# Global attention: two units at a time on every engine, in place of one

## The chip, the cores and the metric

The kernel runs on one NeuronCore of a Trainium2 chip. The metric is the device time of one execution in microseconds, the median of several. The engines, each with its own instruction queue worked strictly in order, are TensorE (PE, with its weight loads PEld), VectorE (DVE), ScalarE (ACT), GpSimd (POOL) and SyncE (SP, which issues transfers here). They meet through semaphores.

## The reference

Four layers follow one another on a tensor of 4 images, 64 x 64 positions, 128 channels. The change concerns the second, a single-head attention of every position over all 4096 positions of its image:

```python
h = group_norm(x, gn_scale, gn_bias)            # 32 groups of 4 channels
hf = h.reshape(B, N, C)                         # N = 4096, C = 128
q, k, v = hf @ wq + bq, hf @ wk + bk, hf @ wv + bv
w_ = jnp.einsum('bqd,bkd->bqk', q, k) * C ** (-0.5)
w_ = jax.nn.softmax(w_, axis=2)
o = jnp.einsum('bqk,bkd->bqd', w_, v)
o = o @ wo + bo
return x + o.reshape(B, H, W, C)
```

The first layer is an attention over 7 x 7 neighbours, the third a gated product with row sums, the fourth a convolution with a selective scan. They run before and after this stage and aren't touched.

## The kernel before

`layer1` computes this attention for four images in one stream. Products of single precision are made from a high and a low part (tiles ending in h and l): `three` (L697 to L700) issues high x high, low x high, high x low.

For each image the queries are 32 blocks of 128. A block's scores over 4096 keys are 8 units of 512 keys, so an image has 256 score units, and all four have STEPS = 1024. The weights have to be turned before they can be multiplied with the values. For that two blocks form a group, and a group has 16 units: unit V turns 256 queries by 256 keys (four transposes, L777) and multiplies them with the values (six matmuls, L789 to L791).

All engines walk through the same list of steps, from -30 to STEPS + 3. In step t there are:

- TensorE: the scores of unit t + 24 into one of three score banks (`psS`), the turn of unit t + 1 into one of two banks (`psT`), the product with the values of unit t. After every 16 steps, in step 16m + 3, two output matmuls (L801).
- VectorE: the maximum of score unit t + 24 (L963, it also copies the scores to `pr`; the last of eight is followed by two small operations for the row), and the low part `pl` of the turned unit t + 1 (L974), which needs the high part. In step 16m + 3 the finish of a group (L981 to L989).
- ScalarE: the high part `ph` of the turned unit t + 1 (L864), then the exponential of unit t + 16 (L869). In step 16m + 1 a copy of the output sums (L875).

A turn waits for `pl` of the unit two before it, a product with the values for its own `pl`, a score for its bank, which the maximum gives back.

Work for the next image stands at the head of certain steps, planned in `at` (L533 to L553), and is done by every engine ahead of the step's own. With base = 256b for image b: the load and turning of a chunk ("raw", "channels") every 22 steps from base - 244 on; the moments of the normalisation in steps base - 66 to base - 62, with a square root on ScalarE; and, for eight chunks each, "norm" (a load), two steps later "normal" (high part `nh` on ScalarE, an affine operation on VectorE, low part `nl` on GpSimd), two steps after that "product". Products of kind 0 give k and q of a chunk, are in the eight steps from base - 26, one in each, and take two score banks. Products of kind 1 give v, are in every second step from base - 14, and take one. In a product TensorE fills a bank, ScalarE makes the high part of k, q or v (`kh`, `qh`, `vh`), VectorE the low part (`kl`, `ql`, `vl`) and gives the bank back. The banks are handed out in the order of use, three in turn (`bank`, L562). `xc` (loads), `nh` and `nl` have two buffers each.

Of the kernel before, what the change touches and what calls it, by code (L numbers as in the profile page):

```python
# [8 lines left out]
ALU = mybir.AluOpType  # L9
# [3 lines left out]
NI = 4  # L13
# [472 lines left out]
def layer1(nc, io, x1, x1t, x2):  # L486
    with ExitStack() as ctx:
# [50 lines left out]
        for b in range(NI):  # L538
# [7 lines left out]
            for kind, first, every in ((0, -26, 1), (1, -14, 2)):  # L546
                for ch in range(8):
# [1 line left out]
                    plan(t, "product", b, ch, kind)  # L549
                    plan(t - 2, "normal", b, ch, kind)  # L550
                    plan(t - 4, "norm", b, ch, kind)
        for jobs in at.values():
            jobs.sort(key=lambda j: ("product", "normal", "channels", "moments", "norm", "raw").index(j[0]))  # L553
        steps = range(-30, STEPS + 4)
        first = [("channels", 0, ch) for ch in range(8)] + [("moments", 0, k) for k in range(3)]


# [40 lines left out]

        for job in first:
            order(job)  # L600
        for step in steps:
            for job in at.get(step, ()):
                order(job)
            if 0 <= step + 24 < STEPS:
                bank("s", step + 24)
        normals = {job[1:]: i for i, job in enumerate(j for s in steps for j in at.get(s, ()) if j[0] == "normal")}
        products = {job[1:]: i for i, job in enumerate(j for s in steps for j in at.get(s, ()) if j[0] == "product")}
        splits = {}
# [85 lines left out]
        def tensor(e):  # L694
# [52 lines left out]
                channels(0, ch)  # L747
            for k in (1, 2):
                fold(0, k)
            for step in steps:  # L750
                for what, *a in at.get(step, ()):
                    if what == "channels":
                        channels(*a)
                    elif what == "moments" and a[1]:
                        fold(*a)
                    elif what == "product":
                        product(*a)
                U = step + 24
                if 0 <= U < STEPS:
                    b, (q, kc) = U // 256, divmod(U % 256, 8)  # L760
                    i = S_use["s", U][1]
                    qs, ks = slice(128 * q, 128 * q + 128), slice(512 * kc, 512 * kc + 512)
                    for ch in (kc, q // 4):
                        _, bk, turn = S_use["q", b, ch]
                        w.wait_ge(S_free[bk], turn + 1)
                    S_wait(w, "s", U)
                    three(psS[:, i, :], qh[:, qs], ql[:, qs], kh[:, ks], kl[:, ks]).then_inc(S_full, 1)
                V = step + 1
                if 0 <= V < STEPS:
                    i, g, j = V % 2, V // 16, V % 16  # L770
                    if V >= 2:
                        w.wait_ge(p_lo, V - 1)
                    for q in range(2):
                        w.wait_ge(exped, 8 * (2 * g + q) + j // 2 + 1)
                        for k in range(2):
                            kt = 2 * j + k
                            t = e.transpose(psT[:, i, 256 * k + 128 * q:256 * k + 128 * q + 128], pr[:, (2 * g + q) % 5, 128 * kt:128 * kt + 128], ident[:])  # L777
                    t.then_inc(T_full, 1)
                if 0 <= step < STEPS:
                    b, j, i, G = step // 256, step % 16, step % 2, step // 16  # L780
                    out = psO[:, G % 2, 0:256]
                    w.wait_ge(p_lo, step + 1)
                    if G >= 2:
                        w.wait_ge(o_out, G - 1)
                    _, bk, turn = S_use["v", b, j // 2]
                    w.wait_ge(S_free[bk], turn + 1)
                    for k in range(2):
                        kt, ks = 2 * j + k, slice(256 * k, 256 * k + 256)
                        e.matmul(out, vh[:, kt, :], ph[:, i, ks], start=(j == 0 and k == 0), stop=False)  # L789
                        e.matmul(out, vl[:, kt, :], ph[:, i, ks], start=False, stop=False)  # L790
                        t = e.matmul(out, vh[:, kt, :], pl[:, i, ks], start=False, stop=(j == 15 and k == 1))  # L791
                    t.then_inc(pv_done, 1)
                if step % 16 == 3 and step > 16:
                    G = step // 16 - 1
                    w.wait_ge(o_out, G + 1)
                    if G:
                        w.wait_ge(y_done, 2 * G)
                    else:
                        w.wait_ge(bob_done, 1)
                    for q in range(2):  # L800
                        t = e.matmul(psF[:, 128 * q:128 * q + 128], ots[:, 128 * q:128 * q + 128], wraw[:, 3, :], start=True, stop=True)  # L801
                    t.then_inc(F_full, 1)

        def scalar(e):
# [40 lines left out]
            for ch in range(8):  # L845
                channels(0, ch)
            root(0)
            for step in steps:
                for what, *a in at.get(step, ()):
# [8 lines left out]
                V = step + 1  # L858
                if 0 <= V < STEPS:
                    i = V % 2  # L860
                    w.wait_ge(T_full, V + 1)
                    if V >= 2:
                        w.wait_ge(pv_done, V - 1)
                    e.activation(ph[:, i, :], psT[:, i, :], ACT.Copy).then_inc(p_hi, 1)  # L864
                Q, k = divmod(step + 16, 8)
                if 0 <= Q < 32 * NI:
                    s, es = Q % 5, slice(512 * k, 512 * k + 512)
                    w.wait_ge(maxed, 2 * Q + 2)
                    e.activation(pr[:, s, es], pr[:, s, es], ACT.Exp, bias=st[:, s, 9:10], scale=SC, accum_out=st[:, s, 10 + k:11 + k]).then_inc(exped, 1)  # L869
                if step % 16 == 1 and step > 16:  # L870
                    G = step // 16 - 1
                    w.wait_ge(pv_done, 16 * G + 16)
                    if G:
                        w.wait_ge(F_full, G + 1)
                    e.activation(ots[:], psO[:, G % 2, 0:256], ACT.Copy).then_inc(o_out, 1)  # L875

        def vector(e):
# [42 lines left out]
            def product(b, ch, kind):  # L920
# [6 lines left out]
                else:  # L927
                    bk, sl4 = S_use["v", b, ch][1], slice(4 * ch, 4 * ch + 4)
                    w.wait_ge(hi_done, splits["v", b, ch] + 1)
                    e.tensor_tensor(vl[:, sl4, :], psS[:, bk, :].rearrange("p (t c) -> p t c", c=128), f32(vh[:, sl4, :]), ALU.subtract).then_inc(S_free[bk], 1)  # L930

            e.memset(zero[:], 0.0)
            w.wait_ge(weights, 192)
            e.tensor_copy(wh[:], wraw[:, 0:3, :]).then_inc(w_hi, 1)
# [5 lines left out]
                channels(0, ch)  # L940
            for k in range(3):
                fold(0, k)
            for step in steps:
                for what, *a in at.get(step, ()):
# [8 lines left out]
                U = step + 24  # L953
                if 0 <= U < STEPS:
                    (Q, kc), ks = divmod(U, 8), slice(512 * (U % 8), 512 * (U % 8) + 512)
                    s = Q % 5
                    u, bk, turn = S_use["s", U]
                    w.wait_ge(S_full, u + 1)
                    if Q >= 5:
                        w.wait_ge(T_full, 16 * ((Q - 5) // 2) + 16)  # L960
                    elif s == 4:
                        w.wait_ge(S_full, 8)
                    e.tensor_tensor_reduce(pr[:, s, ks], psS[:, bk, :], zero[:].broadcast_to([128, 512]), 1.0, -3.0e38,  # L963
                                           ALU.add, ALU.max, st[:, s, kc:kc + 1]).then_inc(S_free[bk], 1)
                    if kc == 7:
                        w.wait_ge(S_free[bk], turn + 1)
                        e.tensor_reduce(st[:, s, 8:9], st[:, s, 0:8], AX.X, ALU.max).then_inc(maxed, 1)
                        w.wait_ge(maxed, 2 * Q + 1)
                        e.tensor_scalar(st[:, s, 9:10], st[:, s, 8:9], -SC, None, ALU.mult).then_inc(maxed, 1)  # L969
                V = step + 1  # L970
                if 0 <= V < STEPS:
                    i = V % 2
                    w.wait_ge(p_hi, V + 1)
                    e.tensor_tensor(pl[:, i, :], psT[:, i, :], f32(ph[:, i, :]), ALU.subtract).then_inc(p_lo, 1)  # L974
                if step % 16 == 3 and step > 16:
                    G = step // 16 - 1
                    for q in range(2):
                        n = 2 * G + q
                        s = n % 5
# [1024 lines left out]
```

## Time and profile before

| | |
|---|---|
| three runs | 4606.60, 4616.47, 4618.91 us; median 4616.47 |
| the profiled execution | 4611.34 us, its span 4609.5 us |
| mean granted clock of TensorE | 0.891 of full speed |
| busy share of the span: PE, DVE, ACT, POOL | 84%, 74%, 58%, 30% |
| this attention, by its first and last product with values | 898.9 to 2909.1 us |

The shares are means over four layers with different limits. What a change in one of them is worth has to be read in that stretch alone, by its waits and its timeline.

### The profile page before, as it was taken

What the parts mean: (1) busy time and instruction counts of PE and PEld (TensorE: products, weight loads), DVE (VectorE), ACT (ScalarE), POOL (GpSimd) and SP (SyncE); (2) the same over time, 40 slices, a digit from 0 to 9 for tenths busy, and PEclk for the clock granted to TensorE, in tenths of its full rate; (3) what the DMA queues carried; (4) which work ended last, traced back from release to release, by engine and by line L of the source; (5) the groups of instructions that cost most, each with busy time, mean ns of one, the idle gap of its engine ahead of it and who ended that gap; (6) DMA issues with size and microseconds to landing.
All of it is one profiled execution on the core that took longest, in us unless ns stands there. A gap on an engine that the chain in (4) does not pass through costs nothing. (4 is left out here: it accounts for less than half of the span.)

```text
span 4609.5 us, 73934 instructions
## 1 busy us (share of the span) xinstructions
PE 3873.8 (84%) x25590; PEld 2996.1 (65%) x25590; DVE 3406.9 (74%) x7889; ACT 2678.2 (58%) x6018; POOL 1391.3 (30%) x1373
## 2 busy tenths in 40 slices
PE   6888887799999999999999999676999644455579
PEld 4666665699988998899888998444666311111148
DVE  4666666577787777777787777695666798899934
ACT  3666665577776777767776667333222466666621
POOL 2434443100010000200010000112244599999910
PEclk9999999799999999999999999898999755555579
DMA  7777774200010000100010000212222311122143
GB/s 205 204 199 198 197 198 137 76 24 21 18 37 27 20 24 16 42 24 24 17 39 13 10 10 10 67 62 95 77 77 71 145 55 55 60 69 71 58 151 102
DMA packets 274687, 346.40 MB, mean 75 GB/s; under 512 B 34954, under 2 KB 159754, under 8 KB 272778
## 3 DMA queue, kind: packets, MB, share of 16 engines
q1 hardware_dynamic: 261738, 320.55, 22.8%
q0 software_dynamic: 12288, 16.92, 1.4%
q8 instruction: 205, 3.36, 0.3%
q10 hardware_dynamic: 288, 4.19, 0.2%
q14 instruction: 168, 1.38, 0.1%
HBM read 209.58 MB, written 130.02 MB: 74 GB/s over the span
## 5 line engine op out<-in xcount | busy, mean ns | idle before, releaser
L864 ACT ACTIVATE l_ph<-l_T 128x512 fp32r<-128x512 f32 x1024 | 612.4, 598 | 547.2 <-PE l_T L777 547.2
L974 DVE TENSOR_TENSOR l_pl<-l_T,l_ph 128x512 fp32r<-128x512 f32 x1024 | 707.3, 691 | 274.9 <-ACT l_ph L864 274.2
L963 DVE CUSTOM_DVE_ANT_0 l_pr<-l_S,l_zero 128x512 f32<-128x512 f32 x1024 | 704.7, 689 | 74.1 <-PE l_S L700 11.2
L869 ACT ACTIVATE l_pr<-l_pr,l_st 128x512 f32<-128x512 f32 x1024 | 731.5, 714 | 1.1 <-DVE l_st L969 1.0
L789 PE MATMUL l_O<-l_ph,l_vh 128*128 128x256 f32 x2048 | 661.7, 323 | 12.2 <-DVE l_pl L974 12.1
L777 PE MATMUL l_T<-l_ident,l_pr 128*128 128x128 f32 x4096 | 612.8, 272 | 0.0
L777 PEld LDWEIGHTS l_T<-l_ident,l_pr 128*128 128x128 f32 x4096 | 507.6, 140 | 136.2
L790 PE MATMUL l_O<-l_ph,l_vl 128*128 128x256 f32 x2048 | 577.9, 282 | 0.0
L791 PE MATMUL l_O<-l_pl,l_vh 128*128 128x256 f32 x2048 | 576.8, 282 | 0.0
L1005 POOL TENSOR_TENSOR l_xs<-l_xs,l_bob 128x128 f32<-128x128 f32 x128 | 57.1, 461 | 1644.7 <-DMA l_xs<-x 1643.6
L1658 PE MATMUL l3b_C<-l_D,l_sel 32*128 32x512 f32 x256 | 216.4, 845 | 384.5 <-DVE l3b_E L1716 384.1
L1658 PEld LDWEIGHTS l3b_C<-l_D,l_sel 32*128 32x128 f32 x256 | 72.4, 283 | 601.4 <-DVE l3b_E L1716 598.2
L698 PE MATMUL l_S<-l_kh,l_qh 128*128 128x512 f32 x1024 | 417.6, 408 | 1.1 <-DVE l_st L963 0.6
L1739 POOL TENSOR_TENSOR l_acc<-l_acc,l3b_E 128x512 f32<-128x512 f32 x256 | 403.4, 1576 | 40.7 <-DVE l3b_E L1716 35.4
L789 PEld LDWEIGHTS l_O<-l_ph,l_vh 128*128 128x128 f32 x2048 | 388.8, 190 | 28.2 <-DVE l_pl L974 24.1
L699 PE MATMUL l_S<-l_kh,l_ql 128*128 128x512 f32 x1024 | 406.8, 397 | 0.0
L700 PE MATMUL l_S<-l_kl,l_qh 128*128 128x512 f32 x1024 | 404.3, 395 | 0.0
L790 PEld LDWEIGHTS l_O<-l_ph,l_vl 128*128 128x128 f32 x2048 | 388.8, 190 | 0.0
L791 PEld LDWEIGHTS l_O<-l_pl,l_vh 128*128 128x128 f32 x2048 | 385.8, 188 | 0.0
L1713 DVE TENSOR_TENSOR_SCAN l3b_du<-l3b_L,l3b_du 128x512 f32<-128x512 f32 x256 | 325.6, 1272 | 23.4 <-POOL l3b_du L1750 20.7
L1695 ACT ACTIVATE l3b_E<-l3b_d 128x512 f32<-128x512 f32 x256 | 153.0, 598 | 237.1 <-PE l3b_d L1664 236.9
L433 DVE CUSTOM_DVE_ANT_0 l_pr<-l_S,l_bm 128x308 f32<-128x308 f32 x512 | 237.2, 464 | 57.5 <-PE l_S L309 47.4
(241 smaller groups left out, 8842.7 us busy)
## 6 DMA issues: line engine op xcount, KB each, us to landing
hls<-l_hl SPq DMA_DIRECT2D x64, 512.0 KB, 4.7
l_qs<-hls SPq DMA_DIRECT2D x96, 256.0 KB, 3.8
l_ks<-hls SPq DMA_DIRECT2D x96, 256.0 KB, 4.0
l_xc<-x1t SPq DMA_DIRECT2D x64, 256.0 KB, 2.7
zs<-l3a_tmp SPq DMA_DIRECT2D x64, 256.0 KB, 2.0
l3b_z<-zs SPq DMA_DIRECT2D x64, 256.0 KB, 2.8
yz<-l3b_z SPq DMA_DIRECT2D x64, 256.0 KB, 2.0
l3c_y<-yz SPq DMA_DIRECT2D x16, 1024.0 KB, 17.1
```

Of the source, the lines that this page charges most:

```text
L698: e.matmul(out, lh, rh, start=True, stop=False)
L699: e.matmul(out, ll, rh, start=False, stop=False)
L700: return e.matmul(out, lh, rl, start=False, stop=True)
L777: t = e.transpose(psT[:, i, 256 * k + 128 * q:256 * k + 128 * q + 128], pr[:, (2 * g + q) % 5, 128 * kt:128 * kt + 128], ident[:])
L789: e.matmul(out, vh[:, kt, :], ph[:, i, ks], start=(j == 0 and k == 0), stop=False)
L790: e.matmul(out, vl[:, kt, :], ph[:, i, ks], start=False, stop=False)
L791: t = e.matmul(out, vh[:, kt, :], pl[:, i, ks], start=False, stop=(j == 15 and k == 1))
L864: e.activation(ph[:, i, :], psT[:, i, :], ACT.Copy).then_inc(p_hi, 1)
L869: e.activation(pr[:, s, es], pr[:, s, es], ACT.Exp, bias=st[:, s, 9:10], scale=SC, accum_out=st[:, s, 10 + k:11 + k]).then_inc(exped, 1)
L963: e.tensor_tensor_reduce(pr[:, s, ks], psS[:, bk, :], zero[:].broadcast_to([128, 512]), 1.0, -3.0e38, ALU.add, ALU.max, st[:, s, kc:kc + 1 ...
L974: e.tensor_tensor(pl[:, i, :], psT[:, i, :], f32(ph[:, i, :]), ALU.subtract).then_inc(p_lo, 1)
L1739: e.tensor_tensor(o, o, turned(tE[:, m % 5, :], n ^ a4), ALU.add).then_inc(added, 1)
```

## The change

Every engine walks through pairs of steps. In a pair p (even) the jobs of both steps come first, then TensorE issues the scores of units p + 24 and p + 25, the products with the values of units p and p + 1, and the turns of units p + 2 and p + 3. VectorE does two maxima, then two low parts; ScalarE two high parts, then two exponentials. The banks are handed out in that order. The output matmuls and the group's finish move from step 16m + 3 to the end of pair 16m + 2, the copy of the sums from step 16m + 1 to pair 16m. SyncE and GpSimd keep their lists of single steps; their own order isn't changed. The inner parts of `scores`, `turn`, `attend` and `maximum` are the lines of before.

```diff
+        pairs = range(-30, STEPS + 4, 2)
+        def jobs(pair):
+            return at.get(pair, []) + at.get(pair + 1, [])
...
-        for step in steps:
-            for job in at.get(step, ()):
+        for pair in pairs:
+            for job in jobs(pair):
                 order(job)
-            if 0 <= step + 24 < STEPS:
-                bank("s", step + 24)
+            for U in (pair + 24, pair + 25):
+                if 0 <= U < STEPS:
+                    bank("s", U)
...
         def tensor(e):
+            for pair in pairs:
+                for what, *a in jobs(pair):
...
-                U = step + 24
-                if 0 <= U < STEPS:
...
-                V = step + 1
-                if 0 <= V < STEPS:
...
-                if 0 <= step < STEPS:
...
-                if step % 16 == 3 and step > 16:
-                    G = step // 16 - 1
+                for U in (pair + 24, pair + 25):
+                    if 0 <= U < STEPS:
+                        scores(U)
+                for V in (pair, pair + 1):
+                    if 0 <= V < STEPS:
+                        attend(V)
+                for V in (pair + 2, pair + 3):
+                    if 0 <= V < STEPS:
+                        turn(V)
+                if pair % 16 == 2 and pair > 16:
+                    G = pair // 16 - 1
...
         def scalar(e):
+                for V in (pair + 2, pair + 3):
...
                     e.activation(ph[:, i, :], psT[:, i, :], ACT.Copy).then_inc(p_hi, 1)
+                for Q, k in (divmod(pair + 16, 8), divmod(pair + 17, 8)):
...
                     e.activation(pr[:, s, es], pr[:, s, es], ACT.Exp, ...).then_inc(exped, 1)
-                if step % 16 == 1 and step > 16:
+                if pair % 16 == 0 and pair >= 16:
...
         def vector(e):
+                for U in (pair + 24, pair + 25):
+                    if 0 <= U < STEPS:
+                        maximum(U)
+                for V in (pair + 2, pair + 3):
+                    if 0 <= V < STEPS:
+                        i = V % 2
+                        w.wait_ge(p_hi, V + 1)
+                        e.tensor_tensor(pl[:, i, :], psT[:, i, :], f32(ph[:, i, :]), ALU.subtract).then_inc(p_lo, 1)
+                if pair % 16 == 2 and pair > 16:
```

## Rows read from the trace of the kernel before

**Rows 1.** Windows: us, busy of PE, PEld, DVE, ACT, POOL, then PE clock, DMA share, GB/s

```profile
898.89:2909.07 2010.18, 1997.97 (x14024) 1795.52 (x14022) 1579.09 (x3828) 1430.76 (x3255) 117.86 (x174) 1.00 0.08 22
1340.27:1346.71 6.44, 6.44 (x41) 5.58 (x39) 6.31 (x15) 6.44 (x13) 2.61 (x2) 1.00 0.22 60
```

**Rows 2.** Waits of weight loads, 898.9 to 2909.1 us: total, times, longest

```profile
PEld l_O L789 <- DVE l_pl L974: 24.1, 51, 1.5
```

**Rows 3.** Timeline of a plain step: start us, us, engine, line, operation

```profile
1552.33 0.60 PE L777 MATMUL l_T<-l_ident,l_pr 128*128 128x128 f32 x4
1552.68 0.36 PE L789 MATMUL l_O<-l_ph,l_vh 128*128 128x256 f32 x1
1552.88 0.28 PE L790 MATMUL l_O<-l_ph,l_vl 128*128 128x256 f32 x1
1552.96 0.60 ACT L864 ACTIVATE l_ph<-l_T 128x512 fp32r<-128x512 f32 x1 [0.56 <-PE l_T L777]
...
1553.45 0.71 ACT L869 ACTIVATE l_pr<-l_pr,l_st 128x512 f32<-128x512 f32 x1
1553.48 0.40 PE L698 MATMUL l_S<-l_kh,l_qh 128*128 128x512 f32 x1
1553.59 0.69 DVE L974 TENSOR_TENSOR l_pl<-l_T,l_ph 128x512 fp32r<-128x512 f32 x1 [0.37 <-ACT l_ph L864]
...
1554.53 0.36 PE L789 MATMUL l_O<-l_ph,l_vh 128*128 128x256 f32 x1
```

**Rows 4.** Costliest groups of the page: count | busy, mean ns | idle before

```profile
L963 DVE CUSTOM_DVE_ANT_0 l_pr<-l_S,l_zero 128x512 f32<-128x512 f32 x1024 | 704.7, 689 | 74.1 <-PE l_S L700 11.2
...
L777 PE MATMUL l_T<-l_ident,l_pr 128*128 128x128 f32 x4096 | 612.8, 272 | 0.0
```

**Rows 5.** Timeline at a group's finish

```profile
1540.68 0.15 DVE L981 TENSOR_REDUCE l_st<-l_st 128x1 f32<-128x8 f32 x1
...
1542.04 0.68 DVE L963 CUSTOM_DVE_ANT_0 l_pr<-l_S,l_zero 128x512 f32<-128x512 f32 x1
...
1542.94 0.60 PE L777 MATMUL l_T<-l_ident,l_pr 128*128 128x128 f32 x4
1543.39 0.39 PE L789 MATMUL l_O<-l_ph,l_vh 128*128 128x256 f32 x1
```

**Rows 6.** Timeline beside products of kind 0

```profile
1341.15 0.69 ACT L836 ACTIVATE l_kh<-l_S,l_cols 128x512 fp32r<-128x512 f32 x1
...
1341.88 0.75 DVE L926 SCALAR_TENSOR_TENSOR l_kl<-l_S,l_cols,l_kh 128x512 fp32r<-128x512 f32 x1
...
1343.14 0.58 ACT L864 ACTIVATE l_ph<-l_T 128x512 fp32r<-128x512 f32 x1
...
1346.36 0.59 ACT L864 ACTIVATE l_ph<-l_T 128x512 fp32r<-128x512 f32 x1
```

**Rows 7.** Timeline beside products of kind 1, in the first image and in a change

```profile
876.38 0.60 ACT L842 ACTIVATE l_vh<-l_S 128x512 fp32r<-128x512 f32 x1 [2.17 <-PE l_S L700]
...
877.71 0.55 DVE L918 TENSOR_SCALAR l_xc<-l_xc,l_gs 128x512 f32<-128x512 f32 x1
...
878.34 1.27 POOL L999 TENSOR_TENSOR l_nl<-l_xc,l_nh 128x512 fp32r<-128x512 f32 x1 [3.60 <-DVE l_xc L918]
...
1381.27 0.19 PEld L789 LDWEIGHTS l_O<-l_ph,l_vh 128*128 128x128 f32 x1 [0.40 <-DVE l_pl L974]
...
1386.72 0.19 PEld L789 LDWEIGHTS l_O<-l_ph,l_vh 128*128 128x128 f32 x1 [0.40 <-DVE l_pl L974]
```

**Rows 8.** Timeline of the last steps

```profile
2880.93 0.38 PE L789 MATMUL l_O<-l_ph,l_vh 128*128 128x256 f32 x1 [0.23 <-DVE l_pl L974]
...
2881.75 0.60 PE L777 MATMUL l_T<-l_ident,l_pr 128*128 128x128 f32 x4
...
2883.76 0.39 PE L789 MATMUL l_O<-l_ph,l_vh 128*128 128x256 f32 x1 [0.22 <-DVE l_pl L974]
```

More of the change, by code:

```diff
@@ L551, in layer1 @@
                     plan(t - 4, "norm", b, ch, kind)
-        for jobs in at.values():
-            jobs.sort(key=lambda j: ("product", "normal", "channels", "moments", "norm", "raw").index(j[0]))
+        for todo in at.values():
+            todo.sort(key=lambda j: ("product", "normal", "channels", "moments", "norm", "raw").index(j[0]))
         steps = range(-30, STEPS + 4)
+        pairs = range(-30, STEPS + 4, 2)
+        def jobs(pair):
+            return at.get(pair, []) + at.get(pair + 1, [])
         first = [("channels", 0, ch) for ch in range(8)] + [("moments", 0, k) for k in range(3)]
@@ L749, in tensor, with scores, turn, attend @@
                 fold(0, k)
-            for step in steps:
-                for what, *a in at.get(step, ()):
+            def scores(U):
+                b, (q, kc) = U // 256, divmod(U % 256, 8)
+                i = S_use["s", U][1]
+                qs, ks = slice(128 * q, 128 * q + 128), slice(512 * kc, 512 * kc + 512)
+                for ch in (kc, q // 4):
+                    _, bk, turn = S_use["q", b, ch]
+                    w.wait_ge(S_free[bk], turn + 1)
+                S_wait(w, "s", U)
+                three(psS[:, i, :], qh[:, qs], ql[:, qs], kh[:, ks], kl[:, ks]).then_inc(S_full, 1)
+            def turn(V):
+                i, g, j = V % 2, V // 16, V % 16
+                if V >= 2:
+                    w.wait_ge(p_lo, V - 1)
+                for q in range(2):
+                    w.wait_ge(exped, 8 * (2 * g + q) + j // 2 + 1)
+                    for k in range(2):
+                        kt = 2 * j + k
+                        t = e.transpose(psT[:, i, 256 * k + 128 * q:256 * k + 128 * q + 128], pr[:, (2 * g + q) % 5, 128 * kt:128 * kt + 128], ident[:])
+                t.then_inc(T_full, 1)
+            def attend(V):
+                b, j, i, G = V // 256, V % 16, V % 2, V // 16
+                out = psO[:, G % 2, 0:256]
+                w.wait_ge(p_lo, V + 1)
+                if G >= 2:
+                    w.wait_ge(o_out, G - 1)
+                _, bk, turn_ = S_use["v", b, j // 2]
+                w.wait_ge(S_free[bk], turn_ + 1)
+                for k in range(2):
+                    kt, ks = 2 * j + k, slice(256 * k, 256 * k + 256)
+                    e.matmul(out, vh[:, kt, :], ph[:, i, ks], start=(j == 0 and k == 0), stop=False)
+                    e.matmul(out, vl[:, kt, :], ph[:, i, ks], start=False, stop=False)
+                    t = e.matmul(out, vh[:, kt, :], pl[:, i, ks], start=False, stop=(j == 15 and k == 1))
+                t.then_inc(pv_done, 1)
+            for pair in pairs:
+                for what, *a in jobs(pair):
                     if what == "channels":
@@ L757, in tensor @@
                         product(*a)
-                U = step + 24
-                if 0 <= U < STEPS:
[L760 to L767, printed above, removed]
@@ L768, in tensor @@
-                V = step + 1
-                if 0 <= V < STEPS:
[L770 to L778, printed above, removed]
@@ L779, in tensor @@
-                if 0 <= step < STEPS:
[L780 to L792, printed above, removed]
@@ L847, in scalar @@
             root(0)
-            for step in steps:
-                for what, *a in at.get(step, ()):
+            for pair in pairs:
+                for what, *a in jobs(pair):
                     if what == "channels":
@@ L857, in scalar @@
                         product(*a)
[L858 to L869, printed above, removed]
[L870 to L871 removed]
+                for V in (pair + 2, pair + 3):
+                    if 0 <= V < STEPS:
+                        i = V % 2
+                        w.wait_ge(T_full, V + 1)
+                        if V >= 2:
+                            w.wait_ge(pv_done, V - 1)
+                        e.activation(ph[:, i, :], psT[:, i, :], ACT.Copy).then_inc(p_hi, 1)
+                for Q, k in (divmod(pair + 16, 8), divmod(pair + 17, 8)):
+                    if 0 <= Q < 32 * NI:
+                        s, es = Q % 5, slice(512 * k, 512 * k + 512)
+                        w.wait_ge(maxed, 2 * Q + 2)
+                        e.activation(pr[:, s, es], pr[:, s, es], ACT.Exp, bias=st[:, s, 9:10], scale=SC, accum_out=st[:, s, 10 + k:11 + k]).then_inc(exped, 1)
+                if pair % 16 == 0 and pair >= 16:
+                    G = pair // 16 - 1
                     w.wait_ge(pv_done, 16 * G + 16)
@@ L930, in product, with maximum @@
                     e.tensor_tensor(vl[:, sl4, :], psS[:, bk, :].rearrange("p (t c) -> p t c", c=128), f32(vh[:, sl4, :]), ALU.subtract).then_inc(S_free[bk], 1)
+            def maximum(U):
+                (Q, kc), ks = divmod(U, 8), slice(512 * (U % 8), 512 * (U % 8) + 512)
+                s = Q % 5
+                _, bk, turn = S_use["s", U]
+                w.wait_ge(S_full, S_use["s", U][0] + 1)
+                if Q >= 5:
+                    w.wait_ge(T_full, 16 * ((Q - 5) // 2) + 16)
+                elif s == 4:
+                    w.wait_ge(S_full, 8)
+                e.tensor_tensor_reduce(pr[:, s, ks], psS[:, bk, :], zero[:].broadcast_to([128, 512]), 1.0, -3.0e38,
+                                       ALU.add, ALU.max, st[:, s, kc:kc + 1]).then_inc(S_free[bk], 1)
+                if kc == 7:
+                    w.wait_ge(S_free[bk], turn + 1)
+                    e.tensor_reduce(st[:, s, 8:9], st[:, s, 0:8], AX.X, ALU.max).then_inc(maxed, 1)
+                    w.wait_ge(maxed, 2 * Q + 1)
+                    e.tensor_scalar(st[:, s, 9:10], st[:, s, 8:9], -SC, None, ALU.mult).then_inc(maxed, 1)
             e.memset(zero[:], 0.0)
@@ L942, in vector @@
                 fold(0, k)
-            for step in steps:
-                for what, *a in at.get(step, ()):
+            for pair in pairs:
+                for what, *a in jobs(pair):
                     if what == "channels":
@@ L952, in vector @@
                         product(*a)
[L953 to L976, printed above, removed]
+                for U in (pair + 24, pair + 25):
+                    if 0 <= U < STEPS:
+                        maximum(U)
+                for V in (pair + 2, pair + 3):
+                    if 0 <= V < STEPS:
+                        i = V % 2
+                        w.wait_ge(p_hi, V + 1)
+                        e.tensor_tensor(pl[:, i, :], psT[:, i, :], f32(ph[:, i, :]), ALU.subtract).then_inc(p_lo, 1)
+                if pair % 16 == 2 and pair > 16:
+                    G = pair // 16 - 1
                     for q in range(2):
```

## The prediction

> **What bounds the kernel now.** I read the busy shares by stretch first, then the waits of TensorE, then single steps in the timeline. Names: S is a score unit (three matmuls of 512 columns, L698 to L700), T a turn (four transposes, L777), A a product with the values (six matmuls of 256 columns, L789 to L791); ph and pl are the high and low part of the turned weights (ScalarE L864, VectorE L974), E an exponential (L869), M a maximum (L963). A "step" is one S, T and A.
>
> In the stage's 2010.18 us TensorE is busy 1997.97 [rows 1], and it waits for pl 24.1 us in 51 waits that the view lists [rows 2]. The busy share alone doesn't say that the stream is dense, so I take a step apart [rows 3]. From A at 1552.68 to the next A at 1554.53 are 1.85 us. T and A together take 1552.33 to 1553.48 = 1.15, which leaves S 0.70. The four transposes take 0.60 in all and one of them 0.27 [rows 4], so they start (0.60 - 0.27)/3 = 0.11 apart and T takes 0.44. That leaves A 0.71, 0.118 for each of six. So three stages of dense issue add up to the step: TensorE is the bound, with nothing idle in a plain step.
>
> **Does the order itself cost anything on TensorE?** This decides whether pairing can save at all. The first A starts at 1552.68, only 0.03 after the last transpose (1552.33 + 3 x 0.11 = 1552.66), and the second matmul of A starts 0.20 after the first instead of 0.12. Read alone, the 0.20 looks like a cost of 0.08 for going from T to A. But 0.03 + 0.20 = 0.23 is what one transpose and one A matmul take anyway (0.11 + 0.12). The first A enters early and the gap behind it pays back. At the rows' digits a change of kind costs 0.00 to 0.01; the other end is the 0.08. I take 0.006, by the sum that closes (two changes in a pair become one, 512 pairs): -3 us.
>
> **Plain pairs.** Let X be the start of T(p+2); T(p+3) follows at X+0.44, S, S at X+0.87 and X+1.57, A(p+2) at X+2.27, A(p+3) at X+2.98, the next T at X+3.70. From [rows 3]: ph starts 0.63 after T, holds ScalarE 0.49; pl starts 0.63 after ph and takes 0.69. So pl(p+2) ends at X+0.63+0.63+0.69 = X+1.95, and A(p+2) could start some 0.06 later: 0.26 to spare. pl(p+3) ends by X+2.6, A(p+3) starts at 2.98. Before, A starts 1554.53 - 1552.33 = 2.20 after its T, so the spare was 0.19: the pair is no tighter. VectorE runs pl, pl until X+2.55, then M, M (0.69 each at most [rows 4]) until X+3.93, and is wanted at X+3.70+1.26 = X+4.96. ScalarE runs ph, ph, E, E: X+0.63, 1.12, 1.61, 2.32 (E 0.71), free at X+3.03. Both are ahead. Cost: 0.
>
> **The row finish of each group** (64 of them): VectorE is held 1542.04 - 1540.68 = 1.36 us [rows 5]; now an A that follows starts 0.45 after its T instead of 0.35, 0.10 lost, plus what follows. In the pair VectorE ends this work and two M at X+2.55+1.36+1.38 = X+5.29, and pl is wanted at X+3.70+0.22 (the two output matmuls)+1.26 = X+5.18: 0.11 late, within the 0.26. The wait goes, -6.4 us for 64. (Where the four transposes of a chunk of the next image fall in such a pair a wait of some 0.2 stays, in either order: 0.)
>
> **Products of the next image, kind 0 (k and q).** There are eight of these in each of three image changes, one per step. They run past the previous image's attention. Here the other engines are the limit too: in 6.44 us, two steps, ScalarE is busy 6.44 and VectorE 6.31 [rows 1]. The product uses two of the three score banks, each bank needing TensorE, ScalarE, VectorE in turn. In a pair the order is k, q, k', q', S, S', A, A, T, T, on three banks. q' needs the bank of k, S' that of k'. ScalarE starts with E, E of the pair before and reaches kh only at X+3.03; then, by [rows 6], kh, qh and nh hold it 1343.14 - 1341.15 = 1.99, so kh' starts at X+5.02. kl' starts 0.73 after kh' and takes 0.75: X+6.50. S' starts at X+6.56, takes 0.70 and after a wait about 0.1 more (its second matmul starts late), then A, A 1.42: the next T is at X+8.78. ScalarE had run out of work at X+7.0 (q'h, n'h) and waits until X+8.78+0.63 for the next T: its next jobs stand behind ph in its queue. Before: 3.22 per step (ph at 1343.14 to ph at 1346.36), 6.44 per two. So +2.34 for each of three pairs; the last pair has no nh: kl' behind ql ends at X+5.9, next T at X+8.18, +1.74. Per image 8.8, three images +26.3. Bounds per image: 0 if ScalarE caught up somehow (the row has it 100% busy, so a gap can't be made good), and +12 if the burst also cost what late loads may add, some 0.8 (about an nh) in each of four pairs. I take the worked-out value. The first image has no ph or E beside these products; I take 0 with 3 us either way, since its waits are on loads.
>
> **The two normal parts ahead of them** (steps -28, -27) fall in one pair: ScalarE holds VectorE back with two nh (some 0.7 each, a third of the 1.99, until X+4.5); the second affine (0.55 [rows 7]) and M, M follow, so pl(p+2) starts near X+6.35 instead of 4.96, less the 0.26 to spare: 1.1 lost, where I count 0.5 for the two steps of before (between none and 1.1). +1.8 us, between -1.5 and +3.3.
>
> **Products of kind 1 (v)**, every second step, so one per pair, 24 beside attention. Before, 5.45 us per pair of steps (1381.27 to 1386.72) with a wait of 0.40 [rows 7], so 5.05 without. The chain v high, nh, affine, nl is now behind two E instead of one: vh at X'+3.03, affine 1.33 later, nl 0.63 after that, 1.27 long: nl is there at X'+6.26, the next v at X'+6.31. v is wanted at X+0.87, and X is X'+5.05 plus the wait w that v itself had: 6.31 = 5.05 + 0.87 + 2w gives w = 0.20 and a pair of 5.25. So 0.20 less, 24 times: -4.8 us. The wait on pl goes and a shorter one on nl takes its place.
>
> **The three table loads** (square root between exponentials): longest wait 1.5 [rows 2], 1.2 in the pair by the same working (0.26 to spare instead of 0.19, and VectorE comes out of pl, pl earlier): -1 us.
>
> **The last 24 steps have no S to cover the turn.** Before, two of them take 2.83 us (2880.93 to 2883.76) [rows 8]: A(V) still runs between T(V+1) and A(V+1). In pairs nothing does: T to its A takes 2.01 (2881.75 to 2883.76), the first A 0.82 with its late second matmul (2880.93 to 2881.75), the second 0.71: 3.54. Twelve pairs: 12 x (3.54 - 2.83) = 8.5, less about 1.5 at the ends (one T of 0.44 is counted in, the group finish no longer adds): +7.
>
> **Sum.** 26.3 + 7 + 1.8 - 1 - 4.8 - 6.4 - 3 = +19.9, so +20 us. The profiled execution took 4611.34 us (span 4609.5, 1.8 around it), which gives 4631. The median of the three timed runs is 4616.47, 5 above it; with that base 4636. I say 4635. The order and the sizes of all other stages stay.
>
> **A rule against the change.** In a plain step 0.44 of 1.85 us are transposes and the granted clock is 1.00 over the whole stage [rows 1, 3], the 2.4 GHz level. The Trainium skill ("TensorE: Matmul & The Clock Gate", Part 4: PE-mode transpose) says that transposes don't count as busy for the clock in the way other matmuls do. The pair puts 0.87 us of them in a row, and in the last 24 steps 1.15 us of waiting behind them: if the clock fell to 1.2 GHz there, T and A would take twice as long, 12 x (0.87 + 1.53) = 29 us more, 4664. By that rule; the trace speaks against it, since the last steps of before, with a third of their time in transposes, kept 2.4 GHz. Chance 0.02.
>
> **Rivals.** (a) The bursts cost little: ScalarE's queue is not as far behind as I count, or loads and maxima shift so that k', q' meet free banks; then 7 + 1.8 stand against savings of 15.2: 4616.5 - 6.4 = 4610. Against it: ScalarE's 6.44 of 6.44. Chance 0.15. (b) The other side: grouping removes real cost on TensorE. If the 0.08 behind T were a cost of changing kind, one less per pair is 512 x 0.08 = 41 us, net -21: 4595. It decides from the point where T+A in a row is longer than its parts by over 0.04; the rows have 0.23 against 0.23. Chance 0.06. (c) Plain pairs are not free: if M, M ahead of pl, or ph(p+3) behind ph(p+2), leave A waiting 0.1 in each of some 480 plain pairs, +48 us: 4684. For it: 0.26 to spare is little. Against: VectorE is free 1.0 us before pl is wanted. Chance 0.09. (d) The pair does half of what I say in the bursts (+13 instead of +26): 4622. Chance 0.13. My forecast: 0.55.
>
> **Chances.** No change can be told within 0.3%, 14 us of 4616: 4603 to 4630. Slower: the forecast's own case nearly whole (its range is 4628 to 4645), (c), the clock: 0.68. Same: (d), most of (a), the edge of the forecast: 0.23. Faster: (b) and a tail of (a): 0.09. The range 4608 to 4658 leaves out (b), (c) and the clock.
>
> **What would show it.** In the profile after: plain pairs of 3.70 us from T to T with no wait of A; in the image changes four pairs of some 8.8, 8.8, 8.8, 8.2 us, ScalarE idle some 2.3 in each before ph, waiting for T; value pairs of 5.25; the last pairs 3.54. I am wrong if plain pairs differ from 3.70 by over 0.03 (15 us over the stage), or if the pairs with k and q take under 7.5.

## The result, and the profile after

The changed kernel takes 4633.6 us (median of 8 runs, 4624.36 to 4644.89), the kernel before 4615.23 us (median of 8, 4605.12 to 4620.09). The ratio is 1.0044, with a 95% interval of 1.003 to 1.0058: slower by 18 us. That is 0.44%, clear of no difference at all, and the interval's lower end lies at the 0.3% that the prediction counts as no change. 4635 was forecast.

The profiled execution of after is its slowest, 4644.89 us with a span of 4643.1, so its 33.6 us above the span of before are more than the medians differ. I compare the stage itself, and it stretch by stretch, by the starts of ph. From ph(0) to ph(1022) the stage takes 2010.30 us before and 2029.85 after: +19.55, where +19.9 was worked out for the whole. This measure leaves out both ends. From the stage's first statistics (812.95 and 816.31) to the end of its last result on VectorE (2911.57 and 2932.95) it is 2098.62 before and 2116.64 after: +18.0. The pairs gain 0.6 ahead of ph(0) and 0.95 behind ph(1022): the last ph starts 0.50 after its neighbour in after and 1.68 in before. The other 15.5 us of the two spans lie in layers whose code is the same (last section).

First the busy times of after by stretch (columns: us of the stretch, busy us and instructions of PE, PEld, DVE, ACT, POOL, granted clock, DMA share, GB/s), beside [rows 1]: the stage up to its last product with values, less its first 0.2 us, one pair with products of kind 0, one plain pair, and the last pairs.

```profile
902.28:2930.44 2028.16, 1992.55 (x14017) 1838.47 (x14016) 1474.52 (x3826) 1373.93 (x3254) 117.82 (x174) 1.00 0.08 22
1345.55:1354.18 8.63, 7.01 (x42) 5.50 (x39) 6.29 (x12) 6.30 (x13) 2.58 (x2) 1.00 0.21 60
1550.98:1554.67 3.69, 3.69 (x28) 3.44 (x27) 3.18 (x10) 2.49 (x7) 0.86 (x2) 1.00 0.46 129
2888.63:2927.65 39.02, 28.73 (x226) 26.16 (x225) 15.34 (x28) 19.22 (x43) 0.92 (x2) 1.00 0.03 8
```

The plain pair is full: PE 3.69 of 3.69. In the pair with products ScalarE, which was busy 6.44 of 6.44, has 6.30 of 8.63, and PE has 7.01. In the last pairs PE has 28.73 of 39.02. The granted clock is 1.00 in all.

The waits of weight loads after, beside [rows 2] (us in total, times, longest):

```profile
PEld l_S L704 <- DVE l_kl L942: 25.6, 21, 1.9
PEld l_O L787 <- DVE l_pl L993: 19.7, 24, 1.2
PEld l_S L704 <- POOL l_nl L1018: 10.3, 18, 1.3
```

Two of the three are new: a product or score for a bank that kl gives back, and a product for nl. What was 24.1 us in 51 waits for pl is 19.7 in 24, with the last pairs in it.

A plain pair, beside [rows 3] (start, us, engine, line, operation, and in brackets the idle time before and who ended it):

```profile
1550.98 1.09 ACT L880 ACTIVATE l_ph<-l_T 128x512 fp32r<-128x512 f32 x2 [1.65 <-PE l_T L774]
1551.61 1.29 DVE L993 TENSOR_TENSOR l_pl<-l_T,l_ph 128x512 fp32r<-128x512 f32 x2 [0.27 <-ACT l_ph L880]
1552.60 0.28 PE L787 MATMUL l_O<-l_ph,l_vh 128*128 128x256 f32 x1
1554.03 1.03 PE L774 MATMUL l_T<-l_ident,l_pr 128*128 128x128 f32 x8
1554.67 1.09 ACT L880 ACTIVATE l_ph<-l_T 128x512 fp32r<-128x512 f32 x2 [1.20 <-PE l_T L774]
```

A stands without a wait, and ph comes again after 3.69. The first pl starts at 1551.61 and one takes 0.69, so it ends at 1552.30, 0.30 ahead of the A at 1552.60. With the 0.06 that the prediction allows for the hand-over, 0.24 is to spare, where 0.26 was worked out.

A pair with products of kind 0, beside [rows 6]:

```profile
1344.75 1.04 PE L774 MATMUL l_T<-l_ident,l_pr 128*128 128x128 f32 x8
1345.39 1.09 ACT L880 ACTIVATE l_ph<-l_T 128x512 fp32r<-128x512 f32 x2 [2.26 <-PE l_T L774]
1347.77 0.68 ACT L852 ACTIVATE l_kh<-l_S,l_cols 128x512 fp32r<-128x512 f32 x1
1348.49 0.75 DVE L942 SCALAR_TENSOR_TENSOR l_kl<-l_S,l_cols,l_kh 128x512 fp32r<-128x512 f32 x1 [1.18 <-ACT l_kh L852]
1349.29 0.50 PE L704 MATMUL l_S<-l_nh,l_wh 128*128 128x512 f32 x1 [1.42 <-DVE l_kl L942]
1349.62 0.69 ACT L852 ACTIVATE l_kh<-l_S,l_cols 128x512 fp32r<-128x512 f32 x1
1351.15 0.51 PE L704 MATMUL l_S<-l_kh,l_qh 128*128 128x512 f32 x1 [0.19 <-DVE l_kl L942]
1353.38 1.03 PE L774 MATMUL l_T<-l_ident,l_pr 128*128 128x128 f32 x8
1354.02 1.09 ACT L880 ACTIVATE l_ph<-l_T 128x512 fp32r<-128x512 f32 x2 [2.33 <-PE l_T L774]
```

With X = 1344.75: kh at X+3.02 (3.03 was worked out), kh' at X+4.87 (5.02), S' at X+6.40 (6.56), the next T at X+8.63 (8.78), ScalarE idle 2.33 ahead of ph (2.3). TensorE's long wait, 1.42, is for q', the second product's last matmuls, on the bank that the first kl gives back.

The last pairs, beside [rows 8]:

```profile
2899.27 1.08 ACT L880 ACTIVATE l_ph<-l_T 128x512 fp32r<-128x512 f32 x2 [1.06 <-PE l_T L774]
2899.90 1.29 DVE L993 TENSOR_TENSOR l_pl<-l_T,l_ph 128x512 fp32r<-128x512 f32 x2 [2.26 <-ACT l_ph L880]
2900.64 0.39 PE L787 MATMUL l_O<-l_ph,l_vh 128*128 128x256 f32 x1 [0.98 <-DVE l_pl L993]
2902.18 1.04 PE L774 MATMUL l_T<-l_ident,l_pr 128*128 128x128 f32 x8
2902.82 1.08 ACT L880 ACTIVATE l_ph<-l_T 128x512 fp32r<-128x512 f32 x2 [1.07 <-PE l_T L774]
```

ph to ph is 3.55 (3.54 was worked out), with TensorE waiting 0.98 for pl in each but one: there, two output matmuls stand between, and the wait is 0.53.

The whole stage by stretches, from the start of ph of the first unit named to that of the last. Rows with "x3" are sums over the three image changes. H2 and H3 are two experiments below. In the first row, some 1 us isn't the work of an edit: the first eight steps take 17.36 us in after and E1 and 16.29 in E2, though these three do the same there. Before (17.07) and after both have the long value, H2 (16.08) and H3 (15.95) the short one.

| stretch of steps | before | after | H2 | H3 |
|---|---|---|---|---|
| 0 to 192, plain with 11 finishes | 367.13 | 365.54 | 363.63 | 365.92 |
| moments, 192 to 198, x3 | 40.46 | 39.05 | 39.20 | 47.14 |
| 198 to 226, x3 | 157.55 | 156.47 | 156.42 | 156.76 |
| two nh, 226 to 230, x3 | 23.65 | 23.46 | 23.46 | 23.67 |
| k and q, 230 to 238, x3 | 78.94 | 103.37 | 81.54 | 79.46 |
| 238 to 242, x3 | 22.34 | 22.12 | 22.12 | 21.88 |
| v, 242 to 258, x3 | 132.25 | 130.77 | 122.35 | 133.36 |
| plain, 258 to 448 and 514 to 704 | 723.17 | 719.38 | 718.12 | 723.15 |
| 770 to 1000 | 433.39 | 430.66 | 430.67 | 433.33 |
| 1000 to 1022, no scores | 31.42 | 39.03 | 31.69 | 31.43 |
| total | 2010.30 | 2029.85 | 1989.20 | 2016.11 |

### The profile page after: what moved, and what is told of

Same layout as the page of the kernel before. It is cut to its first block and busy times, and to the rows that moved or that the text cites. A ratio compares the mean times of both kernels' runs of the same rounds, so it can differ in the third digit from the quotient of the medians.

```text
span 4643.1 us, 73934 instructions
## 1 busy us (share of the span) xinstructions
PE 3880.2 (84%) x25590; PEld 3045.5 (66%) x25590; DVE 3303.4 (71%) x7889; ACT 2620.8 (56%) x6018; POOL 1391.7 (30%) x1373
## 5 line engine op out<-in xcount | busy, mean ns | idle before, releaser
L993 DVE TENSOR_TENSOR l_pl<-l_T,l_ph 128x512 fp32r<-128x512 f32 x1024 | 659.4, 686 | 461.5 <-ACT l_ph L880 461.2
L880 ACT ACTIVATE l_ph<-l_T 128x512 fp32r<-128x512 f32 x1024 | 556.8, 595 | 649.7 <-PE l_T L774 649.7
L957 DVE CUSTOM_DVE_ANT_0 l_pr<-l_S,l_zero 128x512 f32<-128x512 f32 x1024 | 661.5, 683 | 0.5 <-PE l_S L706 0.4
L787 PE MATMUL l_O<-l_ph,l_vh 128*128 128x256 f32 x2048 | 579.3, 283 | 12.3 <-DVE l_pl L993 12.0
L774 PE MATMUL l_T<-l_ident,l_pr 128*128 128x128 f32 x4096 | 530.4, 272 | 0.0
L774 PEld LDWEIGHTS l_T<-l_ident,l_pr 128*128 128x128 f32 x4096 | 459.2, 141 | 0.1
L704 PE MATMUL l_S<-l_kh,l_qh 128*128 128x512 f32 x1024 | 448.7, 438 | 3.0 <-DVE l_kl L942 1.7
L787 PEld LDWEIGHTS l_O<-l_ph,l_vh 128*128 128x128 f32 x2048 | 390.3, 191 | 39.6 <-DVE l_pl L993 19.7
L394 ACT ACTIVATE l_pr<-l_pr,l_st 128x308 f32<-128x308 f32 x512 | 278.0, 547 | 0.5 <-DVE l_st L437 0.5
```

What stands on the lines that cost most here:

```text
L704: e.matmul(out, lh, rh, start=True, stop=False)
```

## The experiments

The experiments but E6 start from the kernel after, and walk through groups of one or two steps (E6 is the kernel before with one edit): `single(s)` says which steps go alone. A step alone has the order of before (score, turn, product; ph, exponential). All compute the full reference. The diffs are cut to the lines that matter, and those of E3 and E5 are put in words. E1 to E6 have one run each, on two chips; their whole times are given for the record, and the argument goes by the stretches.

**E1, the last 24 steps alone.** Does the tail cost what I said, and nothing else?

```diff
-pairs = range(-30, STEPS + 4, 2)
+single = lambda s: s >= STEPS - 24
...
```

> The changed kernel with the last 24 steps in single order again (T(V+1), A(V) in turn). My theory: in pairs nothing stands between T and its A once the scores have ended. So the stretch from ph(1000) to ph(1022), 39.03 us in the changed kernel and 31.42 before, falls back to 31.4 to 32; the rest of the stage is as in the changed kernel. Rival: the end is longer for another reason (the clock, the exponentials that still run): it stays at 38 to 39.

Measured: 1000 to 1022 takes 31.68 us in place of 39.03, and no other stretch of the stage moves by over 0.1. The tail's 7.4 is the pairing of steps that have no score to cover their turn. (One run: 4625.0 us, beside 4613.27 of before.)

**E2, the eight steps with k and q alone.**

```diff
+single = lambda s: 0 <= s and s < STEPS - 256 and s % 256 >= 230 and s % 256 <= 236
...
```

> The changed kernel with single order in the eight steps of each image change that hold a product of kind 0 (k and q), pairs elsewhere. My theory: the burst of two products on three banks, behind two exponentials, is what costs 8.2 us per image. The stretch from ph(230) to ph(238) of an image change falls from 34.5 to 26.3 (as before) plus up to 1 us where single steps go back to pairs. Rival: the cost comes from the low parts or loads of the pairs ahead (steps -30 to -27, still in pairs): over 30 us.

Measured: k and q take 80.94, 26.98 per image, after 34.46 per image in pairs. So 22.4 of the burst's 24.4 us go when these steps are alone, and the rival, over 30 us, is out. The way back into pairs costs 1.67 per image (27.12 in place of 22.12 for 238 to 242, 5.0 in all), more than I expected; net of it 17.4 come back. The profile shows 0.7 of it at once: in the first pair behind, the two products stand right behind the turn that the second of them needs, and it waits.

```profile
1354.49 0.60 PE L787 MATMUL l_T<-l_ident,l_pr 128*128 128x128 f32 x4
...
1356.51 0.38 PE L800 MATMUL l_O<-l_ph,l_vh 128*128 128x256 f32 x1 [0.70 <-DVE l_pl L1003]
```

The rest of the 1.67 I didn't trace. The stage takes 2011.18 (4607.79 us in one run, beside 4613.27 of before).

**E3, the two exponentials behind the jobs.** It tests the first half of the mechanism, ScalarE's queue. ScalarE does the next pair's jobs first, and the exponentials of the pair before only then, ahead of ph.

```diff
+held = ()
 for pair in pairs:
     jobs(pair)
+    exponentials(held)
+    held = (pair, pair + 1)
     high parts of pair + 2, pair + 3
-    exponentials((pair, pair + 1))
```

> The changed kernel with one thing moved: on ScalarE the two exponentials of a pair stand behind the next pair's jobs instead of ahead of them. My theory: in pairs with products of kind 0, kh then starts 1.42 us earlier, and with it kh', kl', S' and the next T: those pairs go from 8.63 to 7.2 to 7.5 us; pairs with v lose their wait on nl: 5.3 to 5.05 on average. Rival: the three banks alone bound the burst (each needs three engines in turn, whatever ScalarE does first): it stays at 8.3 or more.

The timeline of E3 in the same burst:

```profile
1333.99 1.09 ACT L899 ACTIVATE l_ph<-l_T 128x512 fp32r<-128x512 f32 x2 [1.02 <-PE l_T L787]
1335.13 0.69 ACT L865 ACTIVATE l_kh<-l_S,l_cols 128x512 fp32r<-128x512 f32 x1
...
1341.49 1.09 ACT L899 ACTIVATE l_ph<-l_T 128x512 fp32r<-128x512 f32 x2 [1.02 <-PE l_T L787]
```

kh starts 1.14 after ph in place of 2.38, and the pair takes 7.50. k and q take 92.97 in all (103.37 in after); v takes 122.37 (130.77), with pairs of 5.02 to 5.04 but for one of 5.20 and one of 5.47 per image: the exponentials also stood ahead of nh there. In the second and third pair of a burst, moving the exponentials gives back 1.1 of the 2.2 us, and not the rest. The first pair stays at 9.02 to 9.09; the last falls from 8.17 to 6.93. The stretches from 258 to 704 take 1.3 less than in after as well, 0.3 in each of four places, which isn't traced. The stage takes 2008.67 (4605.84 us in one run, beside 4613.27 of before).

**E4 and E6, a fourth score bank, in pairs and in single steps.** The two output matmuls get unused columns of `psO`, and their bank goes to the scores. E4 does this to the kernel after, E6 to the kernel before.

```diff
-psS = P.ps("S", [128, 3, 512])
-psF = P.ps("F", [128, 512])
+psS = P.ps("S", [128, 4, 512])
...
-t = e.matmul(psF[:, 128 * q:128 * q + 128], ...)
+t = e.matmul(psO[:, G % 2, 256 + 128 * q:384 + 128 * q], ...)
```

> The changed kernel with four score banks instead of three (the output product's 256 columns move into the unused half of the banks of the sums). My theory: q' then needs no wait, S waits for kl and S' for ql, by my working at X+4.57 and X+5.27, so the next T is at X+7.4 instead of X+8.6: kind 0 pairs of 7.4 us, ScalarE idle 1.1 instead of 2.3 in each. Plain pairs and v pairs don't change. Rival: ScalarE's two exponentials ahead of kh are the whole cost and banks play no part: 8.6 as before.

> The kernel before with four score banks instead of three, nothing else. A control for the four banks of the pairs: in single order TensorE is never stopped by a bank, so the kind 0 stretches stay at 78.9 us for the three images (ScalarE and TensorE full), and the stage at 2010 us. Rival: the fourth bank also helps single order, so that it isn't the burst that needs it: kind 0 stretches under 77.

```profile
1335.21 0.68 ACT L864 ACTIVATE l_kh<-l_S,l_cols 128x512 fp32r<-128x512 f32 x1
1336.73 0.50 PE L716 MATMUL l_S<-l_kh,l_qh 128*128 128x512 f32 x1 [0.74 <-DVE l_kl L952]
...
1340.31 1.08 ACT L891 ACTIVATE l_ph<-l_T 128x512 fp32r<-128x512 f32 x2 [1.28 <-PE l_T L786]
```

In pairs the bank is worth as much as the order in the second and third pair, and more over the burst (12.3 us of the 24.4, where the order gave 10.4): q' has a bank of its own, only S waits for kl (0.74), ScalarE waits 1.28 for T in place of 2.33, and pairs take 7.95, 7.48, 7.48, 7.47: k and q 91.11. In single steps it is worth nothing (79.00 against 78.94; the stage 2009.53 against 2010.30, a difference that lies in the first eight steps, 17.07 and 16.04). E4's stage takes 2016.43; one run each gives 4612.74 us for E4, beside 4613.27 of before, and 4603.37 for E6, beside a median of 4616.8 of before. So banks were no limit before the pairing, and became one by it. v doesn't change in E4 (130.66): its loss is not one of banks.

**E5, ph, E, ph, E in place of ph, ph, E, E.** The plain pair has, by my working, 0.26 to spare ahead of the first A and some 0.4 ahead of the second (pl(p+3) ends by X+2.6, A(p+3) starts at X+2.98). An exponential between the two high parts delays the second by more than that. It tests the second spare alone.

```diff
 for V, step in ((pair + 2, pair), (pair + 3, pair + 1)):
     high part of V
+    exponential of step + 16
-exponentials of pair + 16, pair + 17
```

> The changed kernel with ScalarE's order in a pair turned from ph, ph, E, E into ph, E, ph, E. My theory of plain pairs: the spare is small. ph(p+3) then starts at X+0.63+0.49+0.71 = X+1.83, its pl ends at X+3.15 and A(p+3), wanted at X+2.98, can start at X+3.21: a wait of 0.23 in each plain pair, 3.92 us instead of 3.69, and over 192 plain steps 387 us instead of 365.5. The whole grows by some 100 us. Rival: the spare is larger than I count (VectorE and ScalarE hand over faster than the rows' starts say): under 0.1 per pair.

The timeline of E5 in a plain pair:

```profile
1461.76 0.60 ACT L892 ACTIVATE l_ph<-l_T 128x512 fp32r<-128x512 f32 x1 [1.53 <-PE l_T L787]
...
1462.96 0.59 ACT L903 ACTIVATE l_ph<-l_T 128x512 fp32r<-128x512 f32 x1
...
1463.58 0.69 DVE L1014 TENSOR_TENSOR l_pl<-l_T,l_ph 128x512 fp32r<-128x512 f32 x1 [0.49 <-ACT l_ph L903]
...
1463.98 0.28 PE L802 MATMUL l_O<-l_pl,l_vh 128*128 128x256 f32 x1
...
1464.33 0.39 PE L800 MATMUL l_O<-l_ph,l_vh 128*128 128x256 f32 x1
1464.55 0.28 PE L801 MATMUL l_O<-l_ph,l_vl 128*128 128x256 f32 x1
```

The second ph starts 1.20 after the first (about 0.5 in after), and its pl ends at 1464.27. The second A starts 0.35 behind the matmul before it instead of 0.12, the 0.23 that was expected; but its second matmul then comes 0.22 behind it instead of 0.12, which my expectation left out. So a plain pair takes 4.02 in place of 3.69, 0.33 more. Over 0 to 192 it is 390.57 in place of 365.54, 0.26 per pair in the mean, since the pairs with a group's finish don't grow (4.17 and 4.16). The stage takes 2158.66, 129 us more, where some 100 were expected (the whole takes 4760.21 us in one run, beside a median of 4616.8 of before). So the plain pairs stood near an edge: 0.71 of delay cost 0.23 of wait, which leaves 0.48 to spare ahead of the second A. The delay that rival (c) asks for would have to be longer. The smaller spare, ahead of the first A, no experiment moves; it is read from the trace of after alone.

**H2, all three in one:** the exponentials behind the jobs, four banks, the last 24 steps alone.

> Pairs, with the three costs taken away together: two exponentials behind the next pair's jobs, four score banks, the last 24 steps in single order. My theory: by the same working kind 0 pairs reach T at X+6.5 (TensorE's own work), v pairs 5.02, the tail 31.7. So the stage takes some 1988 to 1992 us from first to last ph, 18 to 22 less than before: ratio to the kernel before 0.995 to 0.996. Rival: the costs overlap, and with the queue and the banks free the next thing (loads or nl of a burst) holds the kind 0 pairs at 7 or more: 1996.

Measured: 4592.97 us median (4588.41 to 4595.44, 5 runs), before 4616.8 on the same chip (15 runs), ratio 0.9947, interval 0.9935 to 0.996. That is 0.5% faster than before and clear of no difference; after wasn't run beside it, and stood 0.44% above before. The stage takes 1989.20, where 1988 to 1992 was expected. Of the 21.1 us that this is below before, 9.9 are v and 11.3 the plain stretches (1.1 of them the first eight steps); k and q are still 2.6 above before.

```profile
1340.22 1.07 ACT L898 ACTIVATE l_ph<-l_T 128x512 fp32r<-128x512 f32 x2
1341.17 0.69 ACT L864 ACTIVATE l_kh<-l_S,l_cols 128x512 fp32r<-128x512 f32 x1
...
1342.32 0.83 ACT L854 ACTIVATE l_nh<-l_xc,l_gs 128x512 fp32r<-128x512 f32 x1
...
1346.59 1.09 ACT L898 ACTIVATE l_ph<-l_T 128x512 fp32r<-128x512 f32 x2 [0.19 <-PE l_T L786]
```

ScalarE runs through again (6.19 busy of 6.37), and a burst pair takes 6.37 to 6.45 behind the first of 7.84 to 7.96. That first pair took 7.11 before; here TensorE waits 0.84 for nl in it. In the second and third pair E3 and E4 alone come to 7.50 and 7.48, and both together take the whole 2.2 off: a chain (ScalarE's queue) and a resource (banks) that give about 1.1 each.

**H3, the exponentials behind the jobs, in single steps.** If this order is good by itself, the pairs aren't needed for it.

> Single order as in the kernel before, with one thing moved: ScalarE's exponential of a step stands behind the next step's jobs. It asks whether pairs are needed for the gain at all. My theory: v pairs of steps lose part of their wait of 0.40 (5.05 to 5.2 instead of 5.45), kind 0 stays at TensorE's and ScalarE's 6.44, plain steps stay at 1.847 with the waits at each group's finish: 2000 to 2004 us for the stage, ratio 0.997 to 0.999, and slower than pairs with the three costs taken away. Rival: moving the exponentials is worth nothing in single order, since nl isn't late there: 2010.

Measured: 4616.53 us (11 runs), ratio 1.0003, interval 0.9994 to 1.0012: no change, where I had expected a gain. My theory fell. v takes 133.36 in place of 132.25, and the moments 47.14 in place of 40.46. The timeline of a v step in H3:

```profile
1370.47 0.60 ACT L871 ACTIVATE l_vh<-l_S 128x512 fp32r<-128x512 f32 x1 [2.33 <-PE l_S L719]
1370.96 0.81 ACT L855 ACTIVATE l_nh<-l_xc,l_gs 128x512 fp32r<-128x512 f32 x1
...
1371.67 0.71 ACT L892 ACTIVATE l_pr<-l_pr,l_st 128x512 f32<-128x512 f32 x1
...
1372.37 0.58 ACT L899 ACTIVATE l_ph<-l_T 128x512 fp32r<-128x512 f32 x1
...
1373.73 0.39 PE L800 MATMUL l_O<-l_ph,l_vh 128*128 128x256 f32 x1 [0.27 <-DVE l_pl L1005]
```

In a single step the turn stands ahead of the product, so the high part is wanted early in the step; with vh, nh and an exponential ahead of it, ph comes late and A waits for pl. In a pair the turns are the last thing that TensorE does, and ScalarE has the time of two scores and two products for the jobs and the exponentials. That the order pays in pairs (E3) and not in single steps (H3) is measured; this reason for it I read from the timeline of two v steps. The order and the fourth bank together weren't tried in single steps; each alone gives nothing there (H3, E6).

At the moments the exponential stands behind a square root with its two table loads, and ph behind that:

```profile
1259.15 1.28 ACT L892 ACT_TABLE_LOAD   x1
1260.45 0.72 ACT L892 ACTIVATE l_pr<-l_pr,l_st 128x512 f32<-128x512 f32 x1
...
1261.17 0.57 ACT L899 ACTIVATE l_ph<-l_T 128x512 fp32r<-128x512 f32 x1
...
1262.52 0.39 PE L800 MATMUL l_O<-l_ph,l_vh 128*128 128x256 f32 x1 [1.88 <-DVE l_pl L1005]
```

A waits 1.88, where it waits 1.24 to 1.27 in before, and the clock falls behind it (last section).

## Why the prediction was right

The forecast was slower, by 20 us; the medians differ by 18.4 and the stage by 18.0 with both ends (19.55 from ph(0) to ph(1022)). By its steps:

- **Change of kind and group finish** (-3, -6.4, together -9.4): the stretches of the table without moments, nh, products and tail give 1.59 + 1.08 + 0.22 + 3.79 + 2.73 = 9.4 less. A plain pair without a finish takes 3.687 in the mean where two steps took 3.693: 0.006, as taken; the rest of the 9.4 is the finishes, 0.1 each. Rival (b), that the 0.20 behind a turn is a cost, would have given 0.08 per pair and is out: the early start and the gap behind it do cancel.
- **Plain pairs at no cost** held, 3.69 per pair. The spare is as small as worked out: 0.24 ahead of the first A by the trace, 0.48 ahead of the second by E5. Rival (c) fell.
- **k and q** (+26.3): +24.4. The mechanism held in every step, and the instants within 0.16: kh' starts 1.85 behind kh, where the row of before gave 1.99 from kh to ph. The first pair is longer (9.05), the next two shorter (8.63, 8.62), the last 8.17 (8.18 was worked out): 34.46 per image, where 34.52 was worked out. What was off is the base. I took 6.44 for every pair of before from one row, 25.76 per image; before takes 26.31, since its pairs are 7.11, 6.45, 6.44 and 6.31. That is 1.65 of the 1.9 us between forecast and result. E2 shows that it is the pairing of these steps, E3 and E4 that it is both the queue and the banks, at about equal parts in the middle pairs. Rivals (a) and (d) fell with it.
- **The last steps** (+7): +7.6 up to ph(1022), by pairs of 3.55, and +6.7 with the end behind it, which the +7 took in. E1 takes it away alone.
- **Table loads** (-1): -1.4.
- **The first image** (0, 3 us either way): -0.6, from the first statistics to ph(0).
- **The two nh ahead** (+1.8): -0.2 in their own stretch. The delay is there, but TensorE doesn't meet it at A: the pair behind has products in front of its A, and the wait is at nl of the first of them:

```profile
1337.38 0.51 PE L704 MATMUL l_S<-l_nh,l_wh 128*128 128x512 f32 x1 [0.64 <-POOL l_nl L1018]
```

 So it stands in the burst's first pair of 9.05 and is part of the 24.4 there. The two terms together are 28.1 worked out and 24.2 measured.
- **v** (-4.8): -1.5, the term I mis-sized most. The steady pairs alternate between 5.15 and 5.42, mean 5.29, near the 5.25 that I had. But my working took the chain from one v to the next and left out the first v of each image, whose nl has no v before it. It is late by itself:

```profile
1376.87 0.81 ACT L842 ACTIVATE l_nh<-l_xc,l_gs 128x512 fp32r<-128x512 f32 x1
1378.34 1.27 POOL L1018 TENSOR_TENSOR l_nl<-l_xc,l_nh 128x512 fp32r<-128x512 f32 x1 [16.07 <-DVE l_xc L934]
1379.66 0.33 PE L704 MATMUL l_S<-l_wh,l_nh 128*128 128x128 f32 x1 [1.09 <-POOL l_nl L1018]
```

 That pair takes 6.40 where before 5.48 did: 0.9 in each of three images. E3, with the exponentials out of the way of nh, has 5.02 there.

The errors of k and q with nh (-3.9) and of v (+3.3) nearly cancel; that the sum is within 2 us of the stage's 18.0 owes much to this luck. The forecast of 4635 against 4633.6 owes some to luck besides, since layers that the change doesn't touch differ by more than that from run to run (last section).

The rule on transposes that stood against the change didn't come true here: the last pairs have 8 transposes in a row (1.04) with waits of 0.98 behind them, and the granted clock is 1.00 over those 39 us. The Trainium skill ("TensorE: Matmul & The Clock Gate", Part 4: PE-mode transpose) says that transposes don't count as busy for the clock in the way other matmuls do; by that the clock could have fallen here, and the trace does not bear it out in this stretch.

## What to carry to other kernels

Grouping work on an engine that is already full of dense issue gains almost nothing there by itself (0.006 us per pair here). It can hide a wait of its own (0.1 us at each group's finish here), but it makes the hand-over between engines coarser: every buffer that goes round between them (three banks) and every queue in strict order (two exponentials ahead of kh) is felt where the other engines are full too. If it is grouped all the same, move the work with the longest slack (the exponential is wanted many steps later) behind the work that others wait for, give the round one more buffer, and leave alone the steps that have nothing to cover the latency. Try each order in the grouping in which it will run: the same move that paid in pairs did nothing in single steps.

## What the runs showed of the hardware

- **The clock fell behind a wait of 1.88 us.** In H3, behind the wait at the moments, windows of the trace (columns as above; the granted clock is the third figure from the right):

```profile
1256.00:1262.50 6.50, 4.64 (x34) 3.95 (x32) 3.80 (x14) 5.89 (x13) 0.00 (x0) 1.00 0.00 1
1263.10:1266.40 3.30, 3.30 (x16) 2.90 (x14) 2.31 (x8) 0.54 (x2) 0.00 (x0) 0.51 0.09 25
1266.40:1272.00 5.60, 5.60 (x42) 5.05 (x40) 3.79 (x10) 3.89 (x9) 0.92 (x2) 0.98 0.13 35
```

 At 1262.52 TensorE starts again, within 0.6 us it is at 1.2 GHz, for at least the 3.3 us of the second row, and then at 2.4 GHz again. It happens behind the waits of 1.88 to 1.91 in all three image changes of H3, and costs an estimated 3.3 x 0.49 = 1.6 us each of the 2.2 that the moments lose per image; the longer wait is the other 0.6. Nowhere between the first product and the tail's end does the kernel after fall so, with waits up to 1.42 on the products and about 1 in each of the last pairs. No run here has a wait of TensorE between 1.45 and 1.88 from the first ph to the last, so where it turns stays open, and so does whether the length of the wait alone decides.
- **Layers whose code is the same differ by up to 12 us from run to run.** The first statistics of this stage begin at 812.95 in before, 816.31 in after, and between 804.86 and 813.55 in the experiments. From the end of its last result on VectorE to the end of the span it is 1698.0 in before, 1710.2 in after, and 1698.4 to 1710.0 in the experiments. So of the 33.6 us between the two spans 18.0 are the stage, 3.4 the layer before and 12.2 the layers behind. One total can't carry a difference of 10 us here. The stage's own stretches repeat within 0.1 us where an edit doesn't touch them, but for the first eight steps (above).
